# Other slots for the first-layer input stages of batches six to eight in a two-layer attention kernel

## The chip, the cores and the metric

One core of one Trainium2 chip. The metric is the time of one execution on the device in microseconds, the median of several. The profiled execution is a single one with its own time.

## The reference

For 8 batches of 256 rows of 128 features, four residual steps follow each other, each on a layer norm of x over the features:

```
q, k = rope(xn @ Wq.T), rope(xn @ Wk.T);  v = xn @ Wv.T        # 16 heads of 8
s    = (q k^T + 0.1 (q*q)(k*k)^T) / sqrt(8), causal
out1 = softmax(s) v;  out2 = the same with q, k each rotated by half a head
x   += (0.5 (out1+out2) + 0.05 out1*out2*gate) @ Wo.T
x   += relu(xn @ W1 + b1) @ W2 + b2
x   += softmax(q k^T / sqrt(8)) v        # second layer, affine norm, biases, not causal
x   += (silu(xn @ Wg) * (xn @ Wu)) @ Wd  # weights given as integers
```

## The kernel before, in words

The work is cut into 16 phases, numbered 0 to 15: phase i is batch i of the first layer's attention for i under 8, and batch i - 8 of the second layer's after that. A phase has 16 slots, one for each head. Slots are written out by hand: each engine walks over phases and slots in the same order, and in each slot issues what is due in it, in a fixed order. In slot s of phase i TensorE computes the scores of phase i + 1 (L939, L940, for the row maxima), then the shifted scores of phase i (L966, L968, transposed, with the row maximum already in an extra row of the operands). VectorE takes the negated maxima of the scores (L766, L768, tile NM). ScalarE makes the exponential of the shifted scores (L607, tile PB). In the first layer GpSimd cuts the upper triangle to zero in every odd slot (`cut`, L478 and L481). In slots 6, 10 and 14 and in slot 2 of the next phase, TensorE multiplies four slots of P with V (`pv`, L992), which in the first layer waits for the cuts. There are two banks of shifted scores, so those of slot s wait for the exponential of slot s - 2; three banks of scores, so those of a slot wait for the maxima three slots back; eight buffers of P. The maxima of 8 slots are transposed (`max_rows`, L949), copied by ScalarE (L611) and put in place by a transfer. That happens in slot 9 for the first half of the next phase's, and in slot 0 for the second half.

Beside that, each batch of the first layer needs its input stage ahead of its phase. For batches 0 to 2 it is done before phase 0; for batches 3 to 7 the table `STAGE_A` gives the slot of every step, counted from slot 0 of phase 0 (slot 16 is slot 0 of phase 1), by batch number from 0, so that its entry 5 is the sixth batch. The steps: `bn`, mean and variance on VectorE (L702, L706). `norm`, on GpSimd: the reciprocal root (L425 to L428) and the normed rows XN (L435). `xT`, TensorE transposes XN (L889) and ScalarE copies it into XT (L564). `q` and `k`, TensorE projects with the weights and the rotated weights (L903), and VectorE multiplies the result by the rope tables (`product`, L728, tile TQ), which empties the bank. `v`, TensorE (L909), copied by ScalarE (L574, tile VA). `rot_q` and `rot_k`, GpSimd adds the two halves (`rotate`, L444, tile QR). `sq_q` and `sq_k`, ScalarE squares the sum (L569). `hi`, ScalarE casts the sum and the square to 16 bits, twice 128x512 (`high`, L581, tile PR). `lo`, the rest of that cast is taken, twice: on GpSimd for the batches in `POOL_LOW` (`low_pool`, L451), else on VectorE (`low`, L733). A store to scratch memory then follows in the queue of SyncE (L351), and in later phases the stacks of operands are loaded from there. The place of the store in that queue follows from `lo`: in the phase of `lo // 16`, ahead of the stack if `lo % 16` is under 4, else at the end of the phase.

`A_BANK` gives the PSUM bank (6 or 7) of the four results xT, q, k, v of a batch; each user of a bank waits until the one before has been emptied. Within a slot GpSimd first makes its cut, then the parts of the other stages, then the spread of v for the next phase (slot 8, L463), then the input stages. ScalarE has the exponential first, then the other copies, then the input stages by batch: copy of xT, squares, copy of v, high casts. VectorE takes the maxima first, then the other stages, then the input stages.

Each batch also has its later stages, from one phase after its own attention: the turned output (slot 4, L1001), the gate (L502 on GpSimd, L811 on VectorE), its transpose (slot 9, L1008), the output projection (L1014), a norm (slot 12), the feed-forward layer (L1022, L621, L1035) in the phase after, and then the input of the second layer. So phase 0 has none of these, phase 1 those of one batch, and from phase 4 on all are there.

Of the kernel before, what the change touches and what calls it, by code (L numbers as in the profile page):

```python
# [74 lines left out]

STAGE_A = {3: dict(bn=None, norm=None, xT=-8, q=-6, k=-5, v=-3, rot_q=-4, rot_k=-3, sq_q=-4, sq_k=-2, hi=-1, lo=0),
           4: dict(bn=-7, norm=-6, xT=3, q=5, k=6, v=7, rot_q=7, rot_k=8, sq_q=8, sq_k=10, hi=12, lo=14),
           5: dict(bn=2, norm=4, xT=13, q=15, k=17, v=18, rot_q=18, rot_k=20, sq_q=19, sq_k=21, hi=22, lo=24),
           6: dict(bn=12, norm=15, xT=26, q=28, k=29, v=30, rot_q=30, rot_k=32, sq_q=31, sq_k=33, hi=40, lo=42),
           7: dict(bn=31, norm=35, xT=42, q=44, k=45, v=46, rot_q=46, rot_k=52, sq_q=47, sq_k=53, hi=55, lo=57)}  # L80
POOL_LOW = (2, 3, 4, 5)
A_BANK = {3: (6, 6, 7, 6), 4: (6, 6, 7, 6), 5: (6, 7, 6, 7), 6: (6, 6, 7, 6), 7: (6, 6, 7, 6)}


LOADS = {(L, b): (L * B + b - 2, "mid") for L in range(2) for b in range(B) if (L, b) > (0, 1)}
# [38 lines left out]
def bank_uses():  # L124
# [6 lines left out]
    for b, a in STAGE_A.items():  # L131
        uses += [(a[step], k, (name, b)) for name, step, k in zip(("xT0", "q", "k", "v0"), ("xT", "q", "k", "v"), A_BANK[b])]
    for i in range(NPH):
# [17 lines left out]
def program(nc, x, w0, tab, small, w1, wint, ident, masks, out):  # L151
    with ExitStack() as ctx:
# [261 lines left out]
        def _(pool):  # L414
# [24 lines left out]
            def rotate(b, n):  # L439
                pool.wait_ge(*emptied("qk"[n], b))  # L440
                if b >= 2:
                    pool.wait_ge(s_lo, 2 * b - 2)
                p = b % 2
                pool.tensor_tensor(QR[p][:, n, 0], TQ[p][:, n, 0:S], TQ[p][:, n, S:2 * S], ALU.add).then_inc(s_rot, 1)  # L444
# [51 lines left out]
            for i in range(-1, NPH + 2):  # L496
                for s in range(H):
# [33 lines left out]
                    for b, a in STAGE_A.items():  # L531
                        if a["norm"] == H * i + s:
                            norm(0, b)
                        for n, step in enumerate(("rot_q", "rot_k")):
                            if a[step] == H * i + s:
                                rotate(b, n)
                        if a["lo"] == H * i + s and b in POOL_LOW:
                            for n in range(2):
# [149 lines left out]
        def _(dve):  # L688
# [36 lines left out]
            def product(b, n):  # L725
                p, name = b % 2, "qk"[n]
                dve.wait_ge(*filled(name, b))
                dve.tensor_tensor(TQ[p][:, n], psum(name, b)[:, :], TAB[:, n], ALU.mult).then_inc(*empties(name, b))  # L728
# [73 lines left out]
            for i in range(-1, NPH + 2):  # L802
                for s in range(H):
# [40 lines left out]
                    for b, a in STAGE_A.items():  # L844
# [4 lines left out]
                        for n in range(2):  # L849
                            if a["qk"[n]] == H * i + s:  # L850
                                product(b, n)
                        if a["lo"] == H * i + s and b not in POOL_LOW:
                            for n in range(2):
# [349 lines left out]
```

## Time and profile before

| | us |
|---|---|
| median of 3 runs (310.73 to 311.9) | 310.78 |
| the profiled execution | 310.66 |
| its span, first to last instruction | 308.9 |
| TensorE busy | 286.3 (93%) |
| VectorE busy | 247.0 (80%) |
| ScalarE busy | 213.0 (69%) |
| GpSimd busy | 184.2 (60%) |

The granted TensorE clock is full in all parts from phase 0 on. The spans of the rows are those of the profiled execution, whose time is 1.8 us more than its span. A matmul is shown until its modelled end; what it costs TensorE is the time to the next start.

### The profile page before, as it was taken

The numbers are of one execution on the slowest core, as the hardware profiler recorded it, in microseconds if no ns is written. First come the engines' busy times: TensorE is split into PE (matmuls) and PEld (weight loads), VectorE is DVE, ScalarE is ACT, GpSimd is POOL, SyncE is SP. The second block draws the span as 40 slices with busy tenths as digits, with TensorE's granted clock in tenths as the row PEclk, the third lists the DMA queues.
The fourth block names the chain that finished last, engine by engine and source line by source line (L and its number), as shares of the span: only waits on it lengthen the run. The fifth ranks groups of instructions, "written<-read, shape, count | busy, mean of one in ns | idle before, by whom it ended". The sixth has DMA issues, their size and how long they took to land.

```text
span 308.9 us, 8383 instructions
## 1 busy us (share of the span) xinstructions
PE 286.3 (93%) x2820; PEld 204.0 (66%) x2820; DVE 247.0 (80%) x992; ACT 213.0 (69%) x494; POOL 184.2 (60%) x414
## 2 busy tenths in 40 slices
PE   7768998899998999999999999999999999999965
PEld 4545655677676777877687776766676666666545
DVE  7789987787879877676777777679898989896764
ACT  7564685677576768685867768697778767677921
POOL 5576879886786878687778614535455444444210
PEclk9997999999999999999999999999999999999999
DMA  6477427412313121321212011121211111000001
GB/s 190 150 205 172 139 63 214 129 55 65 109 53 101 28 82 55 85 55 41 76 39 62 20 57 28 25 63 29 61 46 51 55 28 43 28 22 2 20 17 36
DMA packets 23691, 21.60 MB, mean 70 GB/s; under 512 B 3712, under 2 KB 20608, under 8 KB 23648
## 3 DMA queue, kind: packets, MB, share of 16 engines
q1 hardware_dynamic: 23648, 21.05, 24.5%
q8 instruction: 23, 0.38, 0.5%
q14 instruction: 20, 0.16, 0.2%
HBM read 13.18 MB, written 7.34 MB: 66 GB/s over the span
## 4 chain that ended last, share of the span: by engine, by line
PE 49%; DVE 23%; POOL 16%; issue 5%; ACT 3%; DMA 2%; POOLq 0%; SPq 0%; ACTq 0%; DVEq 0%
PE bank L992 11%; DVE NM L771 7%; PE bank L966 5%; PE bank L1035 4%; PE bank L1022 4%; PE bank L942 4%; POOL PB L481 3%; PE bank L943 3%; POOL XN L435 3%; PE bank L970 3%; POOL RS L428 3%; DVE JUNK L768 3%; POOL PR L451 2%; PE bank L1081 2%; PE bank L1067 2%
## 5 line engine op out<-in xcount | busy, mean ns | idle before, releaser
L607 ACT ACTIVATE PB<-bank 128x384 f32<-128x384 f32 (+1 forms) x256 | 134.3, 545 | 47.2 <-PE bank L968 23.8
L771 DVE TENSOR_REDUCE NM<-bank 128x2 f32<-128x512 f32 x128 | 83.8, 682 | 19.8 <-PE bank L943 19.4
L966 PE MATMUL bank<-QS,KS 128*128 128x256 f16 x256 | 69.9, 274 | 3.7 <-ACT PB L607 2.7
L992 PE MATMUL bank<-PB,VP 128*32 128x256 f32 (+1 forms) x1024 | 61.7, 358 | 0.3 <-ACT PB L607 0.3
L768 DVE CUSTOM_DVE_ANT_0 JUNK<-bank,MSF 128x256 bf16<-128x256 f32 x128 | 53.6, 419 | 0.0
L766 DVE CUSTOM_DVE_ANT_0 JUNK<-bank,MSF 128x128 bf16<-128x128 f32 x128 | 36.3, 283 | 19.3 <-PE bank L940 18.8
L992 PEld LDWEIGHTS bank<-PB,VP 128*32 128x32 f32 x1024 | 26.7, 109 | 23.2 <-issue 9.0
L481 POOL TENSOR_SCALAR_AFFINE_SELECT PB<-PB 128x512 f32<-128x512 f32 x64 | 41.2, 644 | 0.0
L942 PE MATMUL bank<-KS,QS 96*128 96x256 f16 x128 | 35.2, 275 | 0.4
L940 PE MATMUL bank<-KS,QS 96*128 96x256 f16 x128 | 34.8, 274 | 0.0
L943 PE MATMUL bank<-KS,QS 96*128 96x256 f16 x128 | 34.6, 271 | 0.0
L970 PE MATMUL bank<-QS,KS 128*128 128x256 f16 x128 | 34.3, 271 | 0.0
L966 PEld LDWEIGHTS bank<-QS,KS 128*128 128x128 f16 x256 | 24.6, 96 | 13.5 <-ACT PB L607 10.1
L939 PE MATMUL bank<-KS,QS 96*128 96x128 f16 x128 | 28.5, 224 | 3.7 <-DVE NM L768 2.6
L968 PE MATMUL bank<-QS,KS 128*128 128x128 f16 x128 | 27.8, 217 | 0.0
L478 POOL TENSOR_TENSOR HELD<-EPSC 128x1 f32<-128x1 f32 x64 | 13.1, 205 | 24.3 <-ACT PB L607 24.3
L435 POOL TENSOR_SCALAR XN<-xs,NMN,RS 128x128 f32<-128x128 f32 x54 | 24.2, 460 | 2.8
L425 POOL TENSOR_TENSOR VE<-MV,EPSC 128x2 f32<-128x2 f32 x32 | 6.3, 198 | 32.8 <-DVE MV L706 32.8
L470 POOL CAST HGL<-HG 128x256 f16<-128x256 f32 x15 | 6.0, 400 | 31.9 <-DVE HG L800 31.9
L428 POOL TENSOR_TENSOR RS<-VE,EPSC 128x2 f32<-128x2 f32 x32 | 22.7, 710 | 2.5
L903 PE MATMUL bank<-XT,W 128*128 128x256 f32 x64 | 19.5, 441 | 1.0 <-ACT XT L564 0.6
L939 PEld LDWEIGHTS bank<-KS,QS 96*128 96x128 f16 x128 | 12.5, 98 | 10.5 <-DVE NM L768 5.5
(100 smaller groups left out, 589.7 us busy)
## 6 DMA issues: line engine op xcount, KB each, us to landing
scr<-PR SPq DMA_DIRECT2D x16, 256.0 KB, 2.6
QS<-scr SPq DMA_DIRECT2D x16, 128.0 KB, 2.6
QS<-scr SPq DMA_DIRECT2D x32, 64.0 KB, 2.8
KS<-scr SPq DMA_DIRECT2D x32, 64.0 KB, 2.8
KS<-scr SPq DMA_DIRECT2D x16, 128.0 KB, 3.0
scr<-PR SPq DMA_DIRECT2D x16, 128.0 KB, 1.9
out_x<-xs SPq DMA_DIRECT2D x8, 128.0 KB, 2.0
W<-in_w SPq DMA_DIRECT2D x1, 576.0 KB, 5.0
```

The costliest lines, as they stand in the source:

```text
L481: pool.affine_select(out=pr, in_=pr, compare_op=ALU.is_ge, fill=0.0, base=0, pattern=[[0, 4], [1, P]], channel_multiplier=-1).then_inc(s_c ...
L607: act.activation(PB[:, s % RING, 0:n], scored(i, s)[:, 0:n], ACT.Exp).then_inc(s_e, 1)
L766: dve.tensor_tensor_reduce(JUNK[:, g % 3, 0], o[:, 0:P], MSF[:, 1], -1.0, 3e38, ALU.add, ALU.min, accum_out=m[:, s, 0:1])
L768: dve.tensor_tensor_reduce(JUNK[:, g % 3, 1:3], o[:, P:3 * P].rearrange("q (n k) -> q n k", n=2), MSF[:, :], -1.0, 3e38, ALU.add, ALU.min, ...
L771: dve.tensor_reduce(m[:, s, 0:2], o[:, :].rearrange("q (n k) -> q n k", n=2), AX.X, ALU.max, negate=True).then_inc(s_mx, 1)
L939: pe.matmul(o[:, 0:P], q[:, 0:P], k[:, 0:P], start=True, stop=True)
L940: ins = pe.matmul(o[:, P:3 * P], q[:, P:2 * P], k[:, :], start=True, stop=True)
L942: pe.matmul(o[:, 0:S], q[:, 0:P], k[:, :], start=True, stop=True)
L943: ins = pe.matmul(o[:, S:2 * S], q[:, P:2 * P], k[:, :], start=True, stop=True)
L966: pe.matmul(o[:, 0:S], k[:, 0:P], q[:, :], start=True, stop=True)
L970: ins = pe.matmul(o[:, S:2 * S], k[:, P:2 * P], q[:, :], start=True, stop=True)
L992: ins = pe.matmul(o, v, pr, start=(g % 2 == 0 and kt == 0), stop=True, skip_group_check=True)
```

## The change

The steps of batches 5, 6 and 7 (the sixth to the eighth) go to other slots, mostly earlier ones. In particular q of batch 7 goes from slot 12 of phase 2 to slot 14 of phase 1, its k and v to slots 1 and 3 of phase 2, and its casts from phase 3 to slots 12 and 14 of phase 2. The rests of batch 5 go from GpSimd to VectorE. Some results lie in another of the two banks.

```diff
 STAGE_A = {3: ...
-           5: dict(bn=2, norm=4, xT=13, q=15, k=17, v=18, rot_q=18, rot_k=20, sq_q=19, sq_k=21, hi=22, lo=24),
-           6: dict(bn=12, norm=15, xT=26, q=28, k=29, v=30, rot_q=30, rot_k=32, sq_q=31, sq_k=33, hi=40, lo=42),
-           7: dict(bn=31, norm=35, xT=42, q=44, k=45, v=46, rot_q=46, rot_k=52, sq_q=47, sq_k=53, hi=55, lo=57)}
-POOL_LOW = (2, 3, 4, 5)
-A_BANK = {3: (6, 6, 7, 6), 4: (6, 6, 7, 6), 5: (6, 7, 6, 7), 6: (6, 6, 7, 6), 7: (6, 6, 7, 6)}
+           5: dict(bn=2, norm=4, xT=11, q=13, k=15, v=17, rot_q=16, rot_k=18, sq_q=17, sq_k=19, hi=20, lo=22),
+           6: dict(bn=10, norm=12, xT=20, q=22, k=23, v=24, rot_q=23, rot_k=25, sq_q=24, sq_k=26, hi=40, lo=42),
+           7: dict(bn=20, norm=24, xT=28, q=30, k=33, v=35, rot_q=31, rot_k=34, sq_q=32, sq_k=35, hi=44, lo=46)}
+POOL_LOW = (2, 3, 4)
+A_BANK = {3: (6, 6, 7, 6), 4: (6, 6, 7, 6), 5: (6, 7, 7, 7), 6: (7, 6, 7, 6), 7: (6, 6, 6, 6)}
```

## Rows read from the trace of the kernel before

**Rows 1.** Phases 0 to 4: length, busy us of PE, PEld, DVE, ACT, POOL; clock.

```profile
31.99:45.91 13.92, 13.54 (x137) 9.02 (x136) 11.98 (x77) 9.82 (x27) 11.81 (x26) 1.00 0.40 112
45.91:64.30 18.39, 16.10 (x170) 11.78 (x169) 14.49 (x86) 11.46 (x30) 16.98 (x38) 1.00 0.49 148
64.30:82.35 18.05, 16.93 (x175) 12.82 (x174) 15.20 (x86) 12.39 (x34) 13.47 (x33) 1.00 0.26 75
82.35:99.94 17.59, 16.37 (x174) 12.40 (x175) 14.28 (x84) 12.56 (x33) 12.17 (x32) 1.00 0.28 83
99.94:116.95 17.01, 16.42 (x178) 12.70 (x178) 13.91 (x85) 12.22 (x33) 13.54 (x33) 1.00 0.20 57
```

**Rows 2.** The second half of phase 2: busy times, and two rows of VectorE's timeline.

```profile
73.25:82.75 9.50, 8.58 (x87) 6.47 (x88) 9.37 (x55) 5.58 (x16) 6.14 (x16) 1.00 0.26 81
...
75.24 1.28 DVE L733 TENSOR_TENSOR PR<-QR,PR 128x512 f16<-128x512 f32 x2
...
78.67 0.68 DVE L728 TENSOR_TENSOR TQ<-bank,TAB 128x512 f32<-128x512 f32 x1
```

**Rows 3.** GpSimd's timeline around the start of phase 1: start, length, line [idle before].

```profile
44.17 0.19 POOL L478 TENSOR_TENSOR HELD<-EPSC 128x1 f32<-128x1 f32 x1 [1.27 <-ACT PB L607]
...
44.92 2.40 POOL L451 TENSOR_TENSOR PR<-QR,PR 128x512 f16<-128x512 f32 x2
...
48.02 0.19 POOL L425 TENSOR_TENSOR VE<-MV,EPSC 128x2 f32<-128x2 f32 x1
...
50.10 0.20 POOL L478 TENSOR_TENSOR HELD<-EPSC 128x1 f32<-128x1 f32 x1
...
50.85 0.73 POOL L444 TENSOR_TENSOR QR<-TQ 128x256 f32<-128x256 f32 x1
...
56.06 0.53 POOL L463 COPY VP<-VA 128x128 f32<-128x128 f32 x2
```

**Rows 4.** TensorE's timeline, slot 13 of phase 0 to slot 6 of phase 1.

```profile
42.28 0.39 PE L889 MATMUL bank<-IDF,XN 128*128 128x128 f32 x2
42.50 0.22 PE L939 MATMUL bank<-KS,QS 96*128 96x128 f16 x1
...
44.40 1.13 PE L903 MATMUL bank<-XT,W 128*128 128x256 f32 x4
45.37 0.22 PE L939 MATMUL bank<-KS,QS 96*128 96x128 f16 x1
...
48.10 0.86 PE L992 MATMUL bank<-PB,VP 128*32 128x256 f32 x16
48.89 0.71 PE L909 MATMUL bank<-W,XT 128*128 128x128 f32 x4
49.44 0.22 PE L939 MATMUL bank<-KS,QS 96*128 96x128 f16 x1
...
52.46 0.28 PE L966 MATMUL bank<-QS,KS 128*128 128x256 f16 x1 [0.97 <-ACT PB L607]
```

**Rows 5.** ScalarE's timeline in phase 1: a square and the high casts.

```profile
51.61 0.42 ACT L569 ACTIVATE QR<-QR 128x256 f32<-128x256 f32 x1 [0.93 <-POOL QR L444]
...
53.74 1.12 ACT L581 CAST PR<-QR 128x512 f16<-128x512 f32 x2
```

**Rows 6.** TensorE's timeline: slot 9 and end of phase 2, end of phase 3.

```profile
73.47 0.41 PE L1008 MATMUL bank<-IDF,Z 128*128 128x128 f32 x2 [0.49 <-DVE Z L811]
...
82.42 0.27 PE L949 MATMUL bank<-IDF,NM 128*16 128x128 f32 x1 [0.36 <-DVE NM L768]
...
99.13 0.44 PE L889 MATMUL bank<-IDF,XN 128*128 128x128 f32 x2 [0.86 <-POOL XN L435]
```

**Rows 7.** The eighth batch's rests on VectorE beside a cut of GpSimd, two timelines.

```profile
92.86 1.77 DVE L733 TENSOR_TENSOR PR<-QR,PR 128x512 f16<-128x512 f32 x2
...
92.85 0.64 POOL L481 TENSOR_SCALAR_AFFINE_SELECT PB<-PB 128x512 f32<-128x512 f32 x1
```

**Rows 8.** SyncE's queue: the issue after phase 2's last store.

```profile
81.01 0.33 SPq L342 DMA_DIRECT2D QS<-scr  x1
```

## The prediction

> **What bounds the kernel now.** I first cut the run into phases, at the first exponential of each, and took the busy time of every engine [rows 1]. Phase 4 shows the settled kernel: 17.01 us, TensorE (PE) busy for 16.42, nothing else near it. Phases 0 to 3 last 13.92, 18.39, 18.05 and 17.59 us. They carry the first-layer stages of batches 4 to 8 as well, and are the only ones the change touches. The reader is to see two other limits there. In phase 1 GpSimd (POOL) is busy for 16.98 of 18.39 us, with PE at 16.10. In the second half of phase 2 VectorE (DVE) is busy for 9.37 of 9.50 us [rows 2].
>
> Next, the timelines of POOL, PE and ACT (ScalarE). POOL runs from 44.17 into phase 2 with hardly a gap [rows 3]. It is felt on PE by a detour: the square of a rope sum on ACT waits for POOL's rope sum, 0.93 us, and the exponential queued behind it is then late for PE, 0.97 us [rows 4, 5]. So a rope step costs time whenever ACT reaches the square before POOL has reached the sum. Last, where the phases end: PE waits 0.49 us for the gated product in slot 9 of phase 2, 0.36 us at its end for the last row maximum (DVE), and 0.86 us at the end of phase 3 for a norm of POOL [rows 6].
>
> **Prices**, from a start to the next start. PE: a transposed x 0.22 (42.28 to 42.50), a q or k projection 0.97 (44.40 to 45.37), v 0.55, a group of P times V 0.79 [rows 4]. POOL: a causal cut 0.75, a norm with its rsqrt 2.08, a rope sum 0.7, the spread of v 0.5, the two rests 2.35 [rows 3]. ACT: the two high casts 1.12 in all, a square with its copy-out about 0.35 before the next can go [rows 5]. DVE: two rests 1.28, a rope product 0.68 [rows 2]. With these prices and the waits of the code I walked the new order slot by slot; the starting times below are that walk's, set against the trace's.
>
> **The change part by part, on the clock of the profiled run.**
>
> *Phase 0.* PE takes over the sixth batch's k projection (slot 17 to 15): +0.97. It was waiting little there, so phase 1 starts about 0.7 us later (0.25 us fill a gap, and q waits some 0.3 us for its copy of x). On POOL the seventh batch's norm goes from behind the cut of slot 15 to ahead of the cut of slot 13. It fills the 1.27 us of idle time there, and the remaining 0.8 us pushes cut 13, the fifth batch's rests and cut 15 [rows 3]. Cut 15 releases the last P times V of phase 0, which now starts at 48.10 [rows 4]: I get 48.85, and PE, which would be there at 47.9, waits 0.95.
>
> *Phase 1, slots 1 to 6.* The square of q6 (sixth batch) now stands in slot 1, behind a POOL that reaches its sum at 48.8 to 49.5. ACT stalls about 2 us, the second half of it under PE's own wait; exponential 2 comes at 50.15 and PE loses another 0.55. Then things are better than before: by slot 6 PE is where it was (52.15 against 52.46 in [rows 4]), with the seventh batch's x already turned.
>
> *Phase 1, slots 6 to 15.* The rests of the sixth batch leave POOL (-2.35), the eighth batch's norm (+2.08) and rope q (+0.7) come in. The order is what matters. After exponential 7 POOL has cut 7, rope q of the seventh, the spread of v, the eighth's norm, cut 9, rope k of the seventh: 0.75 + 0.7 + 0.5 + 2.08 + 0.75 + 0.7 = 5.5 us. ACT wants that last sum right after exponential 10, some 3 us after exponential 7. So its square holds exponential 11, and PE, with all it may do first, stands still in slot 13 for about 1.7 us (61.7 against 59.9). That is the largest single term. With x and q of the eighth (0.22 + 0.97) inside phase 1, phase 2's first shifted scores come at 65.0 instead of 63.2.
>
> *Phase 2, first half.* k and v of the eighth (0.97 + 0.55) come in. The transposed maxima wait about 0.5 us because the product of q stands before the last maximum on DVE. The turned output of slot 4 wants the bank in which v now lies, and its copy on ACT stands behind a relu, an evacuation and a square: about 0.6. I reach the gated product of slot 9 at 77.2 where the trace has 73.47; its 0.49 us wait [rows 6] is gone.
>
> *Phase 2, second half.* x, q, k, v of the eighth are gone from PE: 0.22 + 0.97 + 0.97 + 0.55 = 2.7 us. But DVE was the limit [rows 2], and its work hardly changes: two products out (1.36), two rests of the eighth in (1.28). The stretch keeps its 8.95 us, or 8.7 at best, so **the 2.7 us taken off PE here buy nothing, while they were paid for in phases 1 and 2a**. The transposed maxima of phase 3 come at 85.9 instead of 82.42: +3.5.
>
> *Phase 3.* The eighth's rope k, square, high casts and rests are gone. With them the late norm at its end should shrink: from 17.59 to the 17.01 of phase 4 [rows 1], and 0.8 if the 0.86 us wait goes too [rows 6]. I take -0.8; bounds 0 and -1.5.
>
> *The queue of transfers.* The eighth's store moves from the end of phase 3 to the end of phase 2. It stands there ahead of the second half of the next stack, which the queue now issues at 81.01 [rows 8], and of the maxima behind it. It holds them until the rests are done, about 85.7, and issued. They are wanted in slot 8 of phase 3, after 94: cost nothing with 3 us in hand; were this cover gone, up to 2 us. The sixth's store waits for rests that are done sooner: nothing. Phases 4 to 15 are untouched.
>
> **Sum.** +3.5 - 0.8 = +2.7, and I take **2.6** since a slot walk rounds waits up. As a check: work on PE is the same; PE's waits up to slot 9 of phase 2 grow by 2.0 us (0.95 + 0.55 + 1.7 + 0.5 + 0.6, less the 0.97 of [rows 4] and some 1.3 in smaller ones), 2.7 us of work are brought forward without a return, 0.8 come back: +3.9 at worst. The profiled execution took 310.66 us (span 308.9), the median is 310.78, so I forecast 313.4. Bounds of the unknown terms: the wait in slot 13 is 0 to 2.5, the bank and maximum waits 0 to 1.1, phase 3 as above.
>
> **A rule weighed.** The rests of the eighth batch, on DVE beside a cut of POOL, took 1.77 us for the two instead of 1.28: 0.49 more [rows 2, 7]. The sixth batch's will now stand beside a POOL that has no rest at all, so up to that much can be added to either engine; I left it out of the sum. The Trainium skill (SBUF — State Buffer, "Who interferes with whom") says that a VectorE instruction with two SBUF inputs and a GpSimd one that reads SBUF exclude each other, the later one blocking in full. By that rule the sum would be +3.1 and the time 313.9; the trace's 1.77 us agrees with it.
>
> **Rivals.**
> A, faster: POOL's own load decides. From 44.17 to its first cut of phase 2 its work falls by 2.35 + 2.08 - 2.08 - 0.7 = 1.65 us; if PE follows that and phase 3 gives 0.6, it is 308.5. For: 16.98 of 18.39 busy. Against: the idle time that the new order makes on POOL before cut 5, where ACT is late. 0.20.
> B, no change: POOL reaches rope k of the seventh before ACT wants it and v's bank is free in time; without the terms of 1.7 and 0.6 the sum is +0.3, 311.1. For: POOL has 1.5 us of idle time around slots 3 to 5 in my walk, and an error there moves all. Against: 5.5 us behind one exponential. 0.25.
> C, slower by more: the two engines exclude each other in phase 1, each rest delaying a cut by about 0.5 and the waits on ACT with it: +3.6, 314.4. It decides as soon as a rest meets a cut in slot 6. 0.15.
> The forecast itself: 0.40. It ends slower because DVE bounds the stretch that is relieved.
>
> **Numbers.** A measurement of this kernel tells 0.5% (1.55 us) from no change. Slower by more than that: forecast and C, 0.55. Within: B, 0.25. Faster: A, 0.20. The range reaches down into A, leaving half of it (0.10) out, and up past C: 309.2 to 315.0.
>
> **What would show it.** Right: in phase 1 an idle gap of ACT of over 1 us before a square of a rope sum, and one of PE near slot 13 released by an exponential; a phase 1 no shorter than 18.4; DVE busy over 90% in the second half of phase 2, with PE well below; phase 3 near 17.0. Wrong: phase 1 plus phase 2 under 36.4 us, or the two starts of phase 3 within a microsecond of each other; or PE, not DVE, without gaps from slot 9 of phase 2. If phase 4 and later change their 17.0 us, something is at work that I have not seen.

## The result, and the profile after

The changed kernel takes 315.55 us (median of 6 runs, 313.9 to 317.96), against 311.43 us for the kernel before (6 runs): a ratio of 1.0163 with an interval of 1.0124 to 1.0202. It is slower, as forecast. The size was forecast too small: 2.6 us were expected, the medians differ by 4.1. The time lies 0.55 us above the top of the stated range, 315.0. Of the 2.15 us by which it exceeds the forecast of 313.4, the change accounts for 1.5; the other 0.65 is that the kernel before has 311.43 here and not the 310.78 that I started from. Here and below, a ratio is taken over the fast executions alone and a median over all, so the quotient of two medians can differ from the ratio by some tenths of a per cent.

The profiled execution took 317.81 us, 7.15 more than the one of before. Of that, 6.7 us arise up to phase 4, from two things, and 1.2 in the last phase; what lies before slot 9 of phase 0 was 0.8 us shorter. The first table of windows shows the two things: phases 0 to 4 of the kernel after, cut as in [rows 1]; behind the times stand the granted clock, the DMA share and the GB/s.

```profile
30.93:45.76 14.83, 14.18 (x141) 10.08 (x142) 12.78 (x80) 10.04 (x28) 13.71 (x31) 1.00 0.36 105
45.76:65.60 19.84, 16.19 (x166) 11.29 (x164) 15.57 (x84) 11.42 (x32) 16.30 (x36) 1.00 0.44 133
65.60:84.99 19.39, 16.72 (x174) 12.42 (x174) 14.94 (x84) 13.20 (x35) 11.55 (x27) 1.00 0.23 71
84.99:105.84 20.85, 18.69 (x174) 13.81 (x175) 14.23 (x87) 11.61 (x30) 12.74 (x33) 0.84 0.27 68
105.84:122.85 17.01, 16.42 (x178) 12.71 (x178) 13.93 (x85) 12.20 (x32) 13.52 (x33) 1.00 0.21 63
...
87.00:89.00 2.00, 2.00 (x8) 1.52 (x6) 0.64 (x4) 0.73 (x2) 0.80 (x3) 0.50 1.02 212
```

Phases 0, 1 and 2 are longer by 0.9, 1.4 and 1.3 us at a full clock. Phase 3, in which I expected a gain, is longer by 3.3, and there the clock column is new: 0.84 over the phase, because TensorE had 0.50 of its clock (1.2 of 2.4 GHz) for 6.8 us from 85.4. In the last row it is busy for all of the 2.00 us and gets through 8 matmuls. Phase 4 is the settled one again: 17.01 us.

**A common clock for comparisons.** Phase 0 starts between 30.9 us (norm_later) and 33.4 us (before_better) in the profiles of this document, for reasons outside the change. So below I count from the transposed maxima (L949) in slot 9 of phase 0 to three marks: M2 and M3, the transposed maxima with which the stacks of phases 2 and 3 are closed (66.02 and 86.58 here), and E4, the first exponential of phase 4. From E4 on the kernels do the same work, apart from stand_still, which has extra work in phase 5, and before_better, whose phase 4 is longer.

| kernel | M2 | M3 | E4 | half clock before E4 |
|---|---|---|---|---|
| before | 24.61 | 43.39 | 60.91 | none |
| the prediction | 26.9 | 46.9 | 63.6 | not thought of |
| after | 27.82 | 48.38 | 67.64 | 6.8 us in phase 3 |

The row of the prediction comes from its figures on the clock of before: 65.0 instead of 63.2 for phase 2's first shifted scores and 0.5 for the wait behind them, 85.9 for M3, +2.7 for E4.

Now TensorE's waits in the kernel after. The columns are as in [rows 4]: the bracket has the idle time and what ended it.

```profile
48.03 0.86 PE L992 MATMUL bank<-PB,VP 128*32 128x256 f32 x16 [0.82 <-POOL PB L481]
49.83 0.28 PE L966 MATMUL bank<-QS,KS 128*128 128x256 f16 x1 [0.34 <-ACT PB L607]
56.99 0.44 PE L1008 MATMUL bank<-IDF,Z 128*128 128x128 f32 x2 [0.55 <-DVE TQ L728]
61.75 0.28 PE L966 MATMUL bank<-QS,KS 128*128 128x256 f16 x1 [1.40 <-ACT PB L607]
66.02 0.27 PE L949 MATMUL bank<-IDF,NM 128*16 128x128 f32 x1 [0.53 <-DVE NM L768]
71.57 0.63 PE L1001 MATMUL bank<-IDF,OT 128*128 128x128 f32 x4 [0.77 <-ACT VA L574]
...
77.41 0.39 PE L1008 MATMUL bank<-IDF,Z 128*128 128x128 f32 x2
...
84.18 0.44 PE L889 MATMUL bank<-IDF,XN 128*128 128x128 f32 x2 [1.16 <-POOL XN L435]
86.58 0.37 PE L949 MATMUL bank<-IDF,NM 128*16 128x128 f32 x1 [1.63 <-DVE NM L768]
```

The reader is to see my list of waits come back one by one: 0.82 for the last cut of phase 0, 0.34 for exponential 2, 1.40 in slot 13 of phase 1, 0.53 for the maxima, 0.77 for the bank that now holds v. Two are not on my list: 0.55 at 56.99 and the size of the pair at the end of phase 2, 1.16 and 1.63. The 0.49 us of [rows 6] at L1008 in phase 2 are gone, as forecast.

ScalarE's timeline shows where the first ones come from: two squares that stand waiting for GpSimd's rope sum (a third, at 56.95, waits 1.04), with the next exponential behind them.

```profile
48.71 0.42 ACT L569 ACTIVATE QR<-QR 128x256 f32<-128x256 f32 x1 [1.95 <-POOL QR L444]
...
60.90 0.42 ACT L569 ACTIVATE QR<-QR 128x256 f32<-128x256 f32 x1 [2.12 <-POOL QR L444]
```

And GpSimd's timeline shows the train ahead of the last of these sums, without a gap: a rope sum, the spread of v, the eighth batch's norm, a cut, and only at 60.15 the sum.

```profile
56.02 0.89 POOL L444 TENSOR_TENSOR QR<-TQ 128x256 f32<-128x256 f32 x1
56.87 0.52 POOL L463 COPY VP<-VA 128x128 f32<-128x128 f32 x2
...
57.76 0.70 POOL L428 TENSOR_TENSOR RS<-VE,EPSC 128x2 f32<-128x2 f32 x1
58.57 0.87 POOL L435 TENSOR_SCALAR XN<-xs,NMN,RS 128x128 f32<-128x128 f32 x2
...
59.55 0.63 POOL L481 TENSOR_SCALAR_AFFINE_SELECT PB<-PB 128x512 f32<-128x512 f32 x1
60.15 0.72 POOL L444 TENSOR_TENSOR QR<-TQ 128x256 f32<-128x256 f32 x1
```

The second half of phase 2, where TensorE was relieved of 2.7 us, looks as forecast (the order of the columns as in [rows 1]):

```profile
78.45:86.58 8.13, 5.06 (x63) 3.04 (x56) 8.00 (x44) 4.81 (x13) 5.72 (x13) 0.93 0.31 96
```

VectorE is busy for 8.00 of 8.13 us, TensorE for 5.06. The relief did not shorten the stretch.

Last, VectorE and GpSimd, which hold each other up: the rests on VectorE, then two rows of GpSimd's timeline beside the first of them.

```profile
53.01 1.72 DVE L733 TENSOR_TENSOR PR<-QR,PR 128x512 f16<-128x512 f32 x2
...
84.15 1.72 DVE L733 TENSOR_TENSOR PR<-QR,PR 128x512 f16<-128x512 f32 x2
```

```profile
53.03 1.17 POOL L481 TENSOR_SCALAR_AFFINE_SELECT PB<-PB 128x512 f32<-128x512 f32 x1
54.16 1.15 POOL L502 TENSOR_TENSOR ZG<-Y,SM 128x256 f32<-128x256 f32 x1
```

The rests of the sixth and of the eighth batch take 1.72 us each pair instead of 1.28 [rows 2]. The cut beside the sixth's takes 1.17 instead of 0.64 [rows 7], the one beside the eighth's, at 84.23, takes 1.10.

**Two theories to test.** (1) The order of the work costs more than I added up, and the clock adds its part in some executions, after TensorE has stood still. (2) The rival: the clock in phase 3 is a whim of the one profiled execution, and the order alone costs the 2.6 us forecast.

### The profile page after: what moved, and what is told of

The parts are those of the page before. It is cut to its first block, busy times and chain, and to the rows that moved or that the text cites. A ratio compares the mean times of both kernels' runs of the same rounds, so it can differ in the third digit from the quotient of the medians.

```text
span 316.1 us, 8381 instructions
## 1 busy us (share of the span) xinstructions
PE 289.9 (92%) x2820; PEld 205.6 (65%) x2820; DVE 248.5 (79%) x994; ACT 213.1 (67%) x494; POOL 183.4 (58%) x412
## 4 chain that ended last, share of the span: by engine, by line
PE 57%; DVE 22%; POOL 11%; issue 4%; ACT 4%; DMA 2%; POOLq 0%; SPq 0%; ACTq 0%; DVEq 0%
PE bank L992 13%; DVE NM L771 7%; PE bank L966 5%; PE bank L1022 5%; PE bank L1035 5%; PE bank L942 4%; PE bank L943 3%; PE bank L970 3%; PE bank L1067 2%; PE bank L940 2%; POOL RS L428 2%; POOL XN L435 2%; PE bank L1081 2%; POOL PB L481 2%; DVE JUNK L768 2%
## 5 line engine op out<-in xcount | busy, mean ns | idle before, releaser
L992 PE MATMUL bank<-PB,VP 128*32 128x256 f32 (+1 forms) x1024 | 62.4, 361 | 1.1 <-POOL PB L481 0.8
L992 PEld LDWEIGHTS bank<-PB,VP 128*32 128x32 f32 x1024 | 26.9, 110 | 24.5 <-issue 9.6
L481 POOL TENSOR_SCALAR_AFFINE_SELECT PB<-PB 128x512 f32<-128x512 f32 x64 | 41.9, 655 | 0.0
L940 PE MATMUL bank<-KS,QS 96*128 96x256 f16 x128 | 36.0, 284 | 0.0
L942 PE MATMUL bank<-KS,QS 96*128 96x256 f16 x128 | 35.2, 275 | 0.4
L943 PE MATMUL bank<-KS,QS 96*128 96x256 f16 x128 | 34.6, 271 | 0.0
L889 PE MATMUL bank<-IDF,XN 128*128 128x128 f32 x64 | 13.4, 293 | 7.3 <-POOL XN L435 3.0
```

What stands on the lines that cost most here:

```text
L481: pool.affine_select(out=pr, in_=pr, compare_op=ALU.is_ge, fill=0.0, base=0, pattern=[[0, 4], [1, P]], channel_multiplier=-1).then_inc(s_c ...
L940: ins = pe.matmul(o[:, P:3 * P], q[:, P:2 * P], k[:, :], start=True, stop=True)
L942: pe.matmul(o[:, 0:S], q[:, 0:P], k[:, :], start=True, stop=True)
L943: ins = pe.matmul(o[:, S:2 * S], q[:, P:2 * P], k[:, :], start=True, stop=True)
L992: ins = pe.matmul(o, v, pr, start=(g % 2 == 0 and kt == 0), stop=True, skip_group_check=True)
```

## Experiments

All ratios are against the kernel before, run on the same chip. The marks are of one profiled execution each. They say more about a part of the order than the medians do, since the unprofiled runs of one kernel differ by up to 5 us.

**1. The changed kernel once more** (no edit), and with the stand-still filled.

> The changed kernel once more, beside the others, for a second profile and more times. Theory 1 (order of work alone: the waits of the walk, VectorE bound in the second half of phase 2, rests on VectorE excluding GpSimd): about +3 us, and phase 3 near 17.5 us whenever TensorE's granted clock stays full. Theory 2 (the clock): where the granted clock falls to half after the two waits at the end of phase 2, phase 3 is 3 us longer, near 20.9 us, and the time +5 to +6 us. I expect both kinds among the runs, told apart by the granted clock of each: about 0.995 with 314 to 315 us, about 0.975 with 317 to 318 us.

316.36 us (4 runs, 315.27 to 318.4), ratio 1.0177 (1.011 to 1.0244). Windows over it:

```profile
62.00:65.50 3.50, 1.93 (x24) 1.09 (x24) 2.60 (x19) 2.49 (x7) 2.41 (x6) 1.00 0.45 138
65.50:68.90 3.40, 3.40 (x17) 2.52 (x17) 1.67 (x8) 0.91 (x3) 2.22 (x6) 0.50 0.07 17
89.40:92.80 3.40, 3.40 (x17) 2.37 (x19) 1.33 (x9) 0.81 (x3) 1.78 (x5) 0.50 0.86 197
```

TensorE is at half its clock again, twice and for 3.4 us each: once from 2.0 us after the wait of slot 13 (1.43 us, over at 63.50), and once in phase 3. Phases 0 to 3 take 14.61, 21.34, 18.91 and 19.90 us. So phase 3 recurs, with half the length, and the stretch of phase 1 is new: the wait of slot 13 was there in the first profile too and kept its full clock.

> The changed kernel with five more projections' worth of matmuls that nobody reads: two before the transposes that end phase 2 (a wait of 1.16 us) and three before the transposed maxima of phase 3 (1.63 us). They take 0.48 us each, 0.96 and 1.45 us, so they lie inside the waits and no other engine does anything else. If the clock falls because TensorE stands still there, the granted clock stays full in phase 3 in every run, phase 3 takes 17.3 to 17.6 us instead of 20.85, and the time is 313.5 to 314.5 us with little scatter. If the clock falls for another reason (what came before, or chance), nothing changes, and some runs stay at 317 to 318 us.

```diff
+    # in the maxima step of phase i == 3, ahead of the transpose
+    for _ in range(3): pe.matmul(m[:, S:2*S], wq, W0[:, 0:S], start=True, stop=True)
+    # in the xT step of the norm in question: two of the same, then the wait for XN
```

The extra matmuls write into a part of a bank that the step overwrites or leaves unread. 316.0 us (4 runs), ratio 1.0157 (1.0082 to 1.0232). TensorE at the end of phase 2, then the windows of phases 1 to 3:

```profile
82.94 1.08 PE L1128 MATMUL bank<-W 128*128 128x256 f32 x4
84.27 0.44 PE L889 MATMUL bank<-IDF,XN 128*128 128x128 f32 x2 [0.25 <-POOL XN L435]
84.88 1.51 PE L1108 MATMUL bank<-W 128*128 128x256 f32 x6
86.56 0.28 PE L949 MATMUL bank<-IDF,NM 128*16 128x128 f32 x1 [0.17 <-DVE NM L768]
```

```profile
45.79:65.68 19.89, 16.20 (x166) 11.29 (x164) 15.62 (x84) 11.44 (x32) 16.37 (x36) 1.00 0.47 133
65.68:85.07 19.39, 17.67 (x179) 13.34 (x180) 14.94 (x84) 13.22 (x34) 11.57 (x27) 1.00 0.24 71
85.07:103.27 18.20, 17.43 (x180) 13.23 (x180) 14.18 (x87) 11.55 (x30) 12.74 (x33) 1.00 0.32 78
```

The waits of 1.16 and 1.63 us have become 0.25 and 0.17, no later step has moved, and the clock is full throughout: phase 3 takes 18.20 instead of 20.85 us. This gives the two parts apart. **The order alone: E4 at 65.05, +4.14 us over before. The clock in phase 3: 67.64 - 65.05 = 2.6 us on top.**

> The changed kernel with the idle time of TensorE at the end of phase 2 filled by matmuls that nobody reads, once more, for the clock. If standing still there is what lets the granted clock fall in phase 3, the profile again shows it full from phase 0 to phase 14 and phase 3 at 18.2 us. If it was chance, a half clock shows in phase 3 in the second profile (20 to 21 us). The other runs have no trace: were the two waits the only cause, none would be below a mean of 0.984.

The same kernel in a second profile: E4 at 65.01, full clock again. But the medians of the filled kernel (316.0, and 315.87 over 6 runs) are no better than that of the changed kernel (315.55). The runs of the filled kernel have mean clocks of 0.978 to 0.989, those of the changed one 0.973 to 0.995, and its two profiled executions (314.06 and 314.99 us) are among its fastest. What the slower ones lose, and where, is not shown by any trace. The mean clock alone does not tell it: the second profile has a mean of 0.984 with a full clock in all phases, since it lost its clock before phase 0. The fill is a means to read the order by, not a cure.

**2. The rests of the sixth batch.**

> The changed kernel with the sixth batch's rests back on GpSimd, nothing else. If the exclusion of the two engines (rival C) is worth about 1 us in phase 1, the cut of 1.17 us and the gate product of 1.15 us are 0.64 and 0.75 us again, but GpSimd has 2.35 us more to do ahead of the eighth batch's norm, so the wait of ScalarE for the seventh's rope k (2.12 us) grows. By my walk GpSimd's load decides and the kernel gets slower by another 1 us (316 us at full clock); by rival C it gets faster by 0.5 to 1 us.

```diff
-POOL_LOW = (2, 3, 4)
+POOL_LOW = (2, 3, 4, 5)
```

319.2 us, ratio 1.0276 (1.0205 to 1.0348): M2 at 30.73, M3 at 51.29, E4 at 68.00. Phase 1 is 22.75 us, with 6.8 us at half clock from 62.0, just behind a wait of 1.43 us. So M2 is 2.9 us later, and that is again two things: GpSimd, without a gap, comes to the seventh's rope k sum 1.3 us later (23.28 us on the marks' clock instead of 21.95), and the rest comes with the half clock. With the rest of the new order, GpSimd can't keep the rests; this part of the change is right. Without rests on VectorE beside them the cut and the gate product take 0.64 and 0.72 us. But waits of 1.17 and 1.62 us at the end of its phase 2 did not cost the clock: phase 3 takes 18.29 us. A stand-still is followed by half clock in some executions and not in others.

> The changed kernel without the two rests of the sixth batch: VectorE only counts the semaphore on with two tiny clears, and the low halves of that batch are whatever lay there. It prices the rests where they now stand, VectorE time (1.28 us) and exclusion of GpSimd together. By the exclusion (rival C), the cut of 1.17 and the gate product of 1.15 us become 0.64 and 0.75, and slot 13 of phase 1 comes 0.9 to 1.1 us earlier; the second transposed maxima of phase 2 come about 1.1 us earlier (34.0 instead of 35.1 us after the start of phase 0). If the exclusion is harmless, because GpSimd waits for an exponential anyway, less than 0.3 us.

```diff
+        if b == 5:
+            dve.memset(HOLD[:, 8+n:9+n], 0.0).then_inc(s_lo, 1)
+            return
```

This leaves out the rests of the sixth batch (16-bit parts of q and k are missing from its scores). 316.91 us (4 runs), ratio 1.0189 (1.0147 to 1.0232), with 3.4 us at half clock in phase 3. M2 at 27.28 (-0.59 against the changed kernel at 27.87 in the filled profile), M3 at 47.84 (-0.50), and the 0.55 us wait at L1008 is gone; the 1.40 in slot 13 stays. The same two rows of GpSimd's timeline, now without rests beside them:

```profile
54.71 0.63 POOL L481 TENSOR_SCALAR_AFFINE_SELECT PB<-PB 128x512 f32<-128x512 f32 x1
55.31 0.73 POOL L502 TENSOR_TENSOR ZG<-Y,SM 128x256 f32<-128x256 f32 x1
```

They are 0.96 us shorter together than in the kernel after. GpSimd then stands still for 0.37 us, and the train ahead of slot 13 starts 0.54 us earlier. The two rests cost the path about 0.5 us, not their own 1.28 or 1.72. For GpSimd's path that is what the exclusion added. For TensorE's wait of 0.55 us on VectorE this run does not separate the exclusion from the time of the rests themselves.

**3. The eighth batch.**

> The changed kernel with only the rests of the eighth batch (and with them its store) back in slot 9 of phase 3. If VectorE bounds the second half of phase 2, the wait of 1.63 us for the transposed maxima of phase 3 shrinks to about 0.4 us, and the start of phase 3 comes 1.2 us earlier; phase 3 then carries 1.28 us on VectorE again and ends 0.5 us later than phase 4's 17.0, so the order alone gives -0.5 to -0.8 us. If the half clock comes from the wait on TensorE there, it is not granted here in phase 3, and against a changed kernel at 317.8 us this one is 3 us faster still (314 us). If the clock has nothing to do with the wait, it falls here as well.

```diff
-  7: dict(... hi=44, lo=46)
+  7: dict(... hi=44, lo=57)
```

M2 27.88, M3 46.80, E4 63.99; phases 14.91, 19.90, 19.39, 17.13, with a full clock; 316.05 us (4 runs, 312.86 to 317.4), ratio 1.0145 (1.0063 to 1.0226). The rests in slot 14 of phase 2 hold M3 by 1.54 us (48.34 to 46.80). That is most of their 1.72, so VectorE is the limit there. 0.5 of it is given back in phase 3, where they now stand. 1.06 us of the 4.1 hang on these two instructions.

> The changed kernel with the eighth batch's row and banks as they were before, the sixth's and seventh's as changed. If the cost lies in the eighth batch (its norm before the seventh's rope k on GpSimd in phase 1, its projections taken out of a stretch that VectorE bounds), the phases 0 to 3 last 67.5 to 68.5 us together, as before (67.95), against 72.3 in the changed kernel at full clock, and the time is within 1 us of before. If the sixth and seventh batches' slots cost as much by themselves, 70 us.

```diff
-  7: dict(bn=20, norm=24, xT=28, q=30, k=33, v=35, rot_q=31, rot_k=34, sq_q=32, sq_k=35, hi=44, lo=46)
+  7: dict(bn=31, norm=35, xT=42, q=44, k=45, v=46, rot_q=46, rot_k=52, sq_q=47, sq_k=53, hi=55, lo=57)
-A_BANK = {... 7: (6, 6, 6, 6)}
+A_BANK = {... 7: (6, 6, 7, 6)}
```

314.02 us, ratio 1.0096 (1.0058 to 1.0133); E4 62.19. With the whole row of the eighth batch put back, 65.05 - 62.19 = 2.9 of the 4.1 us are gone; 1.3 stay with the other two batches. The clock is full in its phases 0 to 3.

**4. The squares, and both mends together.**

> The changed kernel with the two squares of the seventh batch later on ScalarE (slots 10 and 15 of phase 1 instead of 8 and 10); GpSimd's order stays. If the wait of 1.40 us on TensorE in slot 13 is only ScalarE standing before the square, it is gone, and the next limit is cut 11 on GpSimd, which could then come 0.9 us earlier (that is GpSimd's idle time before it). So the second transposed maxima of phase 2 come 1.0 us earlier after the start of phase 0 (34.1 instead of 35.1 us), phase 3's as well (54.6 instead of 55.6), and the time falls by 1 us. If GpSimd's load is the limit (the norm of the eighth batch), nothing moves at the end of phase 1.

```diff
-  6: dict(... sq_q=24, sq_k=26, ...)
+  6: dict(... sq_q=26, sq_k=31, ...)
```

316.55 us (4 runs), ratio 1.014 (1.0072 to 1.0209); M2 26.80, M3 47.36: -1.07 and -0.98. The 1.40 us wait of slot 13 is gone. What is late next is a cut, by less:

```profile
62.84 0.86 PE L992 MATMUL bank<-PB,VP 128*32 128x256 f32 x16 [0.45 <-POOL PB L481]
```

So the wait was made by the place of the square in ScalarE's order, as forecast, and 1.0 us is its price. Phase 3 had half clock for 6.8 us here too (phase 3: 21.02 us).

> The changed kernel with two repairs: the seventh batch's squares later (slots 10 and 15 of phase 1) and the eighth's rests back in slot 9 of phase 3. If the order costs add up, counted from the first transposed maxima of phase 1 to the first exponential of phase 4 and at full clock: changed kernel 65.0, less 1.0 for the squares, less 1.1 for the rests, 62.9 us, against 60.9 before. No wait of TensorE in the second half of phase 2 but the 1.16 us for the norm, and the time 2 us over before (313 us), with less scatter. If the limit moves (cut 11, then the norm of batch 2), less than the sum comes back.

Experiments 3 (rests in slot 57) and 4 together: 313.85 us (10 runs), ratio 1.0096 (1.0063 to 1.013). The two gains add up, 1.06 and 1.09 us: E4 62.90. Windows of phases 1 and 2:

```profile
47.46:66.61 19.15, 16.15 (x166) 11.29 (x164) 15.88 (x86) 11.65 (x33) 16.59 (x37) 1.00 0.48 138
66.61:85.67 19.06, 16.75 (x175) 12.49 (x176) 14.58 (x85) 13.11 (x35) 11.20 (x28) 1.00 0.30 80
```

Phases 1 and 2 together still take 38.2 us, against 36.4 in [rows 1].

**5. Parts of the change alone.**

> Only the sixth batch's row, its banks and its rests on VectorE are changed, the seventh's and eighth's are as before. GpSimd loses 2.35 us in phase 1 and gains nothing, and the seventh's norm stays at the end of phase 0, so cut 15 of phase 0 isn't pushed by it. Theory 1: phase 0 gets 0.9 us longer by the k projection, phase 1 loses that projection and the waits for GpSimd: phases 0 to 3 together 66.5 to 67.5 us, a gain of about 1 us on before (309.5 us). If the early square of the sixth batch costs what the walk says (ScalarE standing 1 us in slot 1), no gain.

Rows 6 and 7 of the table and their banks as before; only row 5, its banks and POOL_LOW changed. 314.93 us (9 runs), ratio 1.0098 (1.0057 to 1.0139). This was a miss. The seventh's norm, left in slot 15, now stands on GpSimd just ahead of the sixth's rope q, so the square of slot 1 is later than in any other version. TensorE's timeline, then a window:

```profile
53.40 0.28 PE L966 MATMUL bank<-QS,KS 128*128 128x256 f16 x1 [2.40 <-ACT PB L607]
```

```profile
53.50:57.10 3.60, 3.60 (x30) 2.38 (x29) 1.93 (x11) 3.08 (x8) 1.86 (x6) 0.53 0.58 193
```

2.40 us of standing still, and right behind it 3.4 us at half clock. E4 is at 64.08 with that half clock in it, against 62.19 at a full clock in eighth_back, where the seventh batch's row is changed as well. So leaving the seventh's row out gained nothing: the parts of the change do not simply add up.

> The kernel before, with only the sixth batch's squares and high casts later on ScalarE in phase 1 (slots 5, 6, 7 instead of 3, 5, 6). The waits of TensorE of 0.97 and 0.79 us behind late exponentials go; but GpSimd goes on without a gap to the gate product, which the transposes of slot 9 want, so a wait of some 0.5 us for that product stands in their place. If GpSimd bounds phase 1, the second transposed maxima of phase 2 come 0.3 to 0.6 us earlier (24.2 instead of 24.6 us after the first ones of phase 1) and the time moves by less than 0.5 us. If ScalarE's queue was the limit, 1.5 us.

```diff
-  5: dict(... sq_q=19, sq_k=21, hi=22, lo=24)
+  5: dict(... sq_q=21, sq_k=22, hi=23, lo=24)
```

The kernel before, with the squares of the sixth batch later, to remove the 0.97 us wait of [rows 4]. 313.59 us (10 runs), ratio 1.007 (1.0034 to 1.0105), E4 64.08; a miss as well. The reason was on no list. VectorE's gated product met a GpSimd without gaps: first VectorE's row, then GpSimd's timeline, then TensorE.

```profile
55.63 2.57 DVE L811 SCALAR_TENSOR_TENSOR Z<-ZG,Y 128x256 f32<-128x256 f32 x1 [0.30 <-POOL ZG L502]
```

```profile
55.69 0.63 POOL L481 TENSOR_SCALAR_AFFINE_SELECT PB<-PB 128x512 f32<-128x512 f32 x1
56.27 0.52 POOL L463 COPY VP<-VA 128x128 f32<-128x128 f32 x2
56.77 2.44 POOL L451 TENSOR_TENSOR PR<-QR,PR 128x512 f16<-128x512 f32 x2
```

```profile
58.34 0.41 PE L1008 MATMUL bank<-IDF,Z 128*128 128x128 f32 x2 [2.60 <-DVE Z L811]
```

The product takes 2.57 us where it otherwise takes 0.42. By the times it stands through the cut, the two copies and the first of the two subtractions (some 1.2 us each). TensorE waits 2.60 us for it, and has half clock for 3.4 us from 59.1.

> The kernel before, with what this study says should be done: the sixth batch's squares and casts later as in the run beside it, its rests on VectorE (slot 8 of phase 1, nothing else of that batch moved), the eighth's norm three slots later, behind the gate product of slot 6 of phase 2, and its rests from slot 9 to slot 12 of phase 3, behind the statistics of slot 11. Expected at full clock, from the first transposed maxima of phase 1 to the first exponential of phase 4: 60.9 less 0.8 in phase 1 (GpSimd has 2.35 us less), less 0.5 in phase 2 (the wait for the gated product), less 0.6 at the end of phase 3 (the wait of 0.86 us for the norm): 59.0 us, and the time 1.5 to 2 us below before (309 us). If VectorE binds phases 1 and 2 instead, the rests cost what they save there and only the 0.6 us of phase 3 comes.

The edit of before_squares, with the sixth's rests on VectorE and the eighth's `norm=38, lo=60`. 311.6 us (12 runs) against 311.14, ratio 1.001 (0.9975 to 1.0045). The gated product still takes 1.45 us in phase 1. E4 is 60.69, 0.22 before the kernel before; phase 4 gives that back (17.28 us). No difference.

> The kernel before with one number changed: the eighth batch's norm on GpSimd in slot 6 of phase 2, behind the gate product, instead of slot 3. In the run with all repairs phase 2 lost 0.88 us (between the second transposed maxima of phases 2 and 3: 17.9 instead of 18.8 us) while the sixth batch's repair cost 0.66 us in phase 1 and the eighth's later rests 0.27 us in phase 4. If those are independent, this kernel has 17.9 us there, all else as before, and is 0.7 to 0.9 us faster than before (about 310.2 us). If the gain came only because phase 1 ended later, nothing.

```diff
-  7: dict(bn=31, norm=35, ...)
+  7: dict(bn=31, norm=38, ...)
```

The one edit on the kernel before whose cost I could read from a row: the norm of the eighth batch stood, on GpSimd, ahead of the gate in phase 2, and the 0.49 us of [rows 6] came from it. Windows of phases 1 and 2, and TensorE at slot 9:

```profile
44.82:63.16 18.34, 16.07 (x170) 11.76 (x169) 14.46 (x84) 11.45 (x30) 16.93 (x38) 1.00 0.50 149
63.16:80.36 17.20, 16.77 (x175) 12.86 (x174) 14.83 (x86) 12.25 (x34) 13.24 (x33) 1.00 0.25 76
```

```profile
71.70 0.39 PE L1008 MATMUL bank<-IDF,Z 128*128 128x128 f32 x2
```

The wait is gone, and so is one of 0.34 us later in the phase; phase 2 takes 17.20 instead of 18.04 us, E4 is 59.96: -0.95 us. 310.3 us (12 runs, 309.05 to 311.7) against 311.82 (18 runs), ratio 0.9976 (0.9949 to 1.0003). It has the earliest E4 of all versions. In the times the gain is not clear of noise: the interval reaches 1.

**6. The clock by itself.**

> The kernel before with two useless clears of 128x2048 words on VectorE (about 1.8 us each) in slot 6 of phase 5, in the middle of the even stretch where the granted clock has been full in every profile. They make TensorE wait for maxima about 2 to 3 us. If a TensorE that stands still for over 1.4 us is what the fall of the granted clock follows, the profile shows a half clock of 3.4 or 6.8 us starting within 2 us of the end of that wait, and phase 5 is 1.5 to 3 us longer than the wait alone would make it. If the clock fell in phase 3 of the changed kernel for a reason of its own (what other engines or transfers did there), the clock stays full here, and phase 5 is longer by the wait only, 2 to 3 us.

```diff
+    # VectorE, phase 5, slot 6, ahead of the maximum; SPARE is used by nothing else
+    for k in range(2): dve.memset(SPARE[:, 2048*k:2048*(k+1)].bitcast(U32), 0)
```

In a phase that the change doesn't touch, two fills of 1.76 us hold VectorE and so TensorE. 314.67 us (5 runs, 313.42 to 315.14), ratio 1.0101 (1.0062 to 1.0139). TensorE behind them, then windows:

```profile
126.61 0.23 PE L943 MATMUL bank<-KS,QS 96*128 96x128 f16 x1 [1.27 <-DVE NM L769]
127.59 0.41 PE L1012 MATMUL bank<-IDF,Z 128*128 128x128 f32 x2 [0.47 <-DVE Z L815]
```

```profile
126.60:128.30 1.70, 1.22 (x11) 0.88 (x11) 1.70 (x12) 0.65 (x2) 0.57 (x2) 1.00 0.00 0
128.30:131.70 3.40, 3.40 (x27) 2.34 (x26) 1.14 (x7) 0.92 (x4) 1.32 (x2) 0.50 0.27 78
```

Waits of 1.27 and 0.47 us (1.74 in all), and phase 5 takes 20.65 instead of 17.00: +3.65. About half of what a stall costs here comes after it, in 3.4 us at half clock from 128.3. The clock falls 1.7 us after the first of them has ended and 0.7 after the second, when TensorE is working again. This is one execution; none of the other 15 profiles has a half clock anywhere between 100 and 299 us.

Theory (2) falls on both counts. The half clock of phase 3 goes with the waits: of five profiles with both waits at the end of phase 2 (1.16 and 1.63 us), four have a half clock in phase 3 (after, again, no_rests, squares_late) and one has not (rests_back); of the four in which these waits were filled or one of them removed (filled, filled_again, eighth_rests_late, two_fixes), none has. And the order alone costs more than 2.6: 4.1 us by the filled profiles.

## Why the prediction was half right

**Phase 0**: right. The 0.95 us wait for cut 15 was 0.82, and the P times V behind it came at 9.83 us after the zero of the marks, where the walk had 9.82.

**Phase 1, slots 1 to 6**: right. ScalarE stood for 1.95 us (about 2), TensorE lost 0.34 (0.55).

**Phase 1, slots 6 to 15**: right in kind and nearly in size. 1.40 against 1.7 us, and squares_late shows the mechanism. But it comes 0.9 us later than I had it (61.75 is 23.55 on the marks' clock, my 61.7 is 22.67), since 0.55 of the wait at L1008, made by the sixth's rests, lies before it. The other 0.3 is no single row. M2 was 27.87 at a full clock where the prediction has 26.9.

**Phase 2, first half**: right, 0.53 and 0.77 against 0.5 and 0.6. The gated product came at 39.21, the walk had 38.17: the 1.0 us from phase 1, carried along.

**Phase 2, second half**: the mechanism held exactly (8.00 of 8.13 us busy on VectorE). From slot 9 to M3 it took 86.58 - 77.41 = 9.17 us instead of my 8.7: the eighth's rests at 1.72 instead of 1.28 are 0.44 of the 0.47. "The 2.7 us taken off PE here buy nothing" stands.

**Phase 3**: the -0.8 came out to the tenth where the clock was full: from M3 to E4 17.52 us before, 16.71 filled. But the sign "phase 3 near 17.0" did not come even at a full clock: counted from exponential to exponential, phase 3 took 18.20, because 1.5 us of the stretch before M3 now lie in it. And nothing here, nor anywhere in the prediction, reckoned with the granted clock: 2.6 us in the profile after, 1.7 in the second (19.90 against 18.20).

**The queue of transfers**: right. The store held the queue until the rests were done, the next stack was issued from 86.37 on, and no matmul of phase 3 waited for a transfer.

**Sum.** The first step that failed is "I left it out of the sum", under **A rule weighed**. The exclusion of VectorE and GpSimd is worth up to 1.0 us here: 0.5 in phase 1, where no_rests took out the rests with it, and 0.44 in phase 2, by the duration of the rests. The rule of the Trainium skill (SBUF — State Buffer, "Who interferes with whom"), that a VectorE instruction with two SBUF inputs and a GpSimd one that reads SBUF exclude each other, agrees with these traces: one price is a cut at 1.17 instead of 0.64, another a pair of rests at 1.72 instead of 1.28. I had an observed 1.77 in [rows 7] for one of the two places and counted the undisturbed 1.28 of the other instead. With it the sum is 3.6, which is rival C's figure, and the order alone measured 4.1. Some 0.5 us of phase 1 and 2 stay unassigned. The second step is the clock, which the prediction put at nothing and which lifts single executions by 2 to 3 us more. The medians differ by 4.1 us; how much of that is clock can't be said, since the kernel before loses it in some of its runs too (309.8 to 311.5 us at a mean clock of 0.994, 311.9 to 314.4 at 0.978). At the highest mean clock the order shows by itself: the two executions of the changed kernel at 0.995, 315.23 and 313.9 us, lie about 4 us above 310.6 us, the median of those of the kernel before at 0.994.

Rival A fell: TensorE did not follow GpSimd's load, although that load went down (16.98 to 16.30 us in phase 1). Rival B needed both waits absent, and both came.

## What to carry to other kernels

Relieving an engine pays only in a stretch that it bounds; read the second busiest engine of that very stretch before moving work into another. Place a step that waits (here a square in front of an exponential) by what its producer has queued ahead of it, not by how soon its input might be there, and price each two-input operation of VectorE at the duration that it had beside GpSimd, not at its best one. In a kernel whose TensorE is busy for over 90% of the time, a stall of 1 to 2 us can cost twice its length, by the half clock that followed it in some of these executions.

## What the runs showed that I had not expected

**Half clock in the middle of a busy kernel.** Around waits of 1.2 to 2.6 us TensorE got 0.50 of its clock, in pieces of 3.4 us or 6.8 us. Most began up to 2 us after it had resumed; in after, no_rests and squares_late the clock fell within the second of the two waits that end phase 2, that of 1.62 to 1.63 us: after (6.8 us), again (3.4 twice), rests_back (6.8), squares_late (6.8), no_rests, sixth_alone, before_squares and stand_still (3.4 each). But waits of the same length left it full: 1.40 to 1.43 us in slot 13 in five of six profiles (all but again), 1.17 and 1.62 in rests_back. What decides between them is open. So is what becomes of the clock at the very end: phase 15 took 25.5 us in the profile before and 26.8 in the one after, with 3.4 us at half clock from 307.3, and the two kernels do the same there. Of the 16 profiles 8 have such a piece near the end, norm_later (from 299.8) among them and the kernel before not.

**A VectorE instruction that stood through several of GpSimd.** 2.57 us instead of 0.42 for the gated product, beside four instructions of GpSimd that followed each other without a gap. That it was passed over by each of them is read from the times; no run took one of the four out. A price for "one beside one", like the 0.49 us of [rows 7], is no upper bound.
